# High and low half of the values side by side in attention's value product, on one Trainium2 core

## The reference, cut to what matters

```
q = rms_norm(x @ Wq + bq, gq).reshape(b, -1, n, d)        # b 8, 256 queries, n 16 heads, d 32
k_img = rms_norm(ctx_img @ Wk_img + bk_img, gk_img).reshape(b, -1, n, d)   # 256 keys
v_img = (ctx_img @ Wv_img + bv_img).reshape(b, -1, n, d)
probs = softmax(einsum('bqnd,bknd->bnqk', q, k_img) * scale)
img_x = einsum('bnqk,bknd->bqnd', probs, v_img)
out = img_x.reshape(b, -1, n * d) @ Wo + bo
```

## Time and profile before

| | |
|---|---|
| median of 3 executions | 1144.49 us (1142.92 to 1145.18) |
| profiled execution, its own time | 1142.49 us |
| its span, first to last instruction | 1140.7 us |
| mean granted TensorE clock | 0.942 |
| attention | about 490 to 712 us of the span |

### The profile page before, as it was taken

The page is one execution under the profiler, slowest core; times in us unless marked ns, Lnnn a source line. Parts: engine busy times, 40 slices in busy tenths (PEclk is TensorE's granted clock), DMA queues, the critical chain, the costliest instruction groups (busy, mean ns, idle before and its releaser), DMA issues. The chain is left out here.

```text
span 1140.7 us, 24592 instructions
## 1 busy us (share of the span) xinstructions
PE 1028.6 (90%) x9092; PEld 771.4 (68%) x9175; DVE 844.8 (74%) x1480; ACT 684.5 (60%) x1203; POOL 582.4 (51%) x635
## 2 busy tenths in 40 slices
PE   5899997789997998868999988789898899999997
PEld 5677775634443776457888766587675788888884
DVE  5589999779998788757888876598756555655548
ACT  4665773779986656567888864484444355545431
POOL 5444445424554445348888786303884355555520
PEclk9999999789999999969999999658999899999998
DMA  8584431869885223222222210564796477678879
GB/s 318 185 255 123 166 110 30 159 191 230 227 223 166 92 67 110 71 80 57 58 57 59 70 43 2 203 263 170 207 273 224 167 239 243 232 250 276 308 265 355
DMA packets 133705, 194.60 MB, mean 171 GB/s; under 512 B 67990, under 2 KB 70204, under 8 KB 132792
## 3 DMA queue, kind: packets, MB, share of 16 engines
q1 hardware_dynamic: 117256, 149.45, 42.5%
q0 software_dynamic: 8544, 24.68, 6.9%
q10 hardware_dynamic: 7792, 18.96, 5.1%
HBM read 127.47 MB, written 44.48 MB: 151 GB/s over the span
## 5 line engine op out<-in xcount | busy, mean ns | idle before, releaser
L470 PE MATMUL ps_y<-kv,toep 128*128 128x288 f32 x640 | 156.5, 407 | 3.2 <-DMA toep<-taps_padded 2.1
L470 PEld LDWEIGHTS ps_y<-kv,toep 128*128 128x128 f32 x640 | 121.2, 190 | 37.9 <-DMA toep<-taps_padded 3.5
L164 POOL TENSOR_TENSOR kv<-kx 128x1024 f32<-128x1024 f32 x32 | 60.6, 1895 | 83.7 <-DVE outT L524 37.6
L1798 DVE TENSOR_REDUCE at_negmax<-ps_s 128x4 f32<-128x1024 f32 x64 | 78.1, 1221 | 32.0 <-PE ps_s L1849 31.3
L2674 POOL DMA_INDIRECT expert_results<-e_yo,target x47 | 68.6, 1459 | 57.5 <-ACT e_yo L2725 57.5
L1141 PEld LDWEIGHTS ps_eg<-e_xT,e_w 128*128 128x128 bf16 x1128 | 69.0, 100 | 14.9 <-issue 2.4
L1141 PE MATMUL ps_eg<-e_xT,e_w 128*128 128x128 bf16 x1128 | 73.1, 223 | 3.8 <-DVE e_xT L2786 3.8
L1141 PE MATMUL ps_eu<-e_xT,e_w 128*128 128x128 bf16 x1128 | 71.5, 220 | 0.0
L2779 DVE COPY e_w<-expert_weights 128x4096 bf16 x47 | 57.7, 1227 | 17.9 <-issue 17.9
L2792 DVE SCALAR_TENSOR_TENSOR e_y<-ps_eu,e_bias,e_y 128x128 f32<-128x128 f32 x94 | 28.7, 347 | 55.5 <-PE ps_eu L1141 53.6
L2669 POOL DMA_INDIRECT e_rows<-token_rows,token x45 | 43.7, 971 | 50.4 <-PE ps_ex L2876 44.5
(11 more groups left out here) (450 smaller groups left out, 3089.0 us busy)
## 6 DMA issues: line engine op xcount, KB each, us to landing
e_parts<-down_parts SPq DMA_DIRECT2D x47, 512.0 KB
w_raw<-in_L_ffn_w ACTq DMA_DIRECT2D x32, 512.0 KB, 4.3
toep<-taps_padded SPq DMA_DIRECT2D x32, 256.0 KB, 3.6
f_draw<-in_L_ffn_rw SPq DMA_DIRECT2D x16, 512.0 KB, 4.3
down_parts<-f_dparts SPq DMA_DIRECT2D x16, 512.0 KB, 2.9
expert_weights<-expert_results SPq DMA_DIRECT2D x16, 512.0 KB, 11.1
x_res<-in_x SPq DMA_DIRECT2D x4, 1024.0 KB
c_in<-in_ctx SPq DMA_DIRECT2D x4, 1024.0 KB, 14.5
```

Source lines behind the costliest of these rows:

```text
L164: pool.tensor_tensor(pairs[:, :, :, 0:HD0], x[:, :, 0:HD0].unsqueeze(2).broadcast_to([P, ROWS_N, WIDE, HD0]), sliding_rows(x, 0, 1, WIDE), ...
L470: last = pe.matmul(y[:, l * B:(l + 1) * B, :, WIDE - 1:], toep[h % 2][:, (DC - 1 - l + m) * P:(DC - l + m) * P], kv[h % 2][:, m * B:(m + 1 ...
L1798: dve.tensor_reduce(negmax[u % 2][:, :].rearrange("p (j q) -> p j q", j=2), psS[:, :, :, :], AX.X, ALU.max, negate=True).then_inc(max_read, 1)
```

## The change

v_hi and v_lo become the two halves of one tile `v_parts` (per head 33 columns high, 33 columns low). The products ph by v_hi and ph by v_lo become one product of 66 columns into a wider ps_o (4 x 2 x 33); pl by v_hi goes into the high half alone. A unit has 8 products of 66 and 8 of 33 columns instead of 24 of 33. VectorE's scaling now covers both halves (4 x 2 x 32) and writes a float32 tile in SBUF, `o_halves`. A second tensor_tensor ("the add") waits for it and adds the two halves into o. TensorE waits for the scaling (`o_scaled`), and the turning of the output still waits for the last write into o (`o_read`).

```diff
-        psO = ctx.enter_context(nc.psum_tensor("ps_o", [P, 4, VC], F32))
+        psO = ctx.enter_context(nc.psum_tensor("ps_o", [P, 4, 2, VC], F32))
+        o_halves = sb("at_ohalves", [P, 4, 2, HD], F32)
...
-                    link(dve.reciprocal(rden[:, :], psO[:, :, HD]))
+                    link(dve.reciprocal(rden[:, :], psO[:, :, 0, HD]))
+                    dve.tensor_tensor(o_halves[:, :, :, :], psO[:, :, :, 0:HD],
+                                      rden[:, :].unsqueeze(2).unsqueeze(3).broadcast_to([P, 4, 2, HD]), ALU.mult).then_inc(o_scaled, 1)
+                    dve.wait_ge(o_scaled, g - 1)
                     out = o[ob % 2][:, :, uo * 2 * HD:(uo + 1) * 2 * HD].rearrange("p q (j d) -> p j q d", j=2)
-                    dve.tensor_tensor(out, psO[:, :, 0:HD].rearrange("p (j q) d -> p j q d", j=2),
-                                      rden[:, :].rearrange("p (j q) -> p j q", j=2).unsqueeze(3).broadcast_to([P, 2, 2, HD]),
-                                      ALU.mult).then_inc(o_read, 1)
+                    halves_of = lambda i: o_halves[:, :, i, :].rearrange("p (j q) d -> p j q d", j=2)
+                    dve.tensor_tensor(out, halves_of(0), halves_of(1), ALU.add).then_inc(o_read, 1)
...
                 if g:
-                    pe.wait_ge(o_read, g)
+                    pe.wait_ge(o_scaled, g)
                 for j in range(2):
                     for q in range(2):
                         cols = slice(q * P, (q + 1) * P)
-                        for n, (pr, vv) in enumerate(((ph, v_hi), (ph, v_lo), (pl, v_hi))):
-                            for kc in range(2):
-                                last = pe.matmul(psO[:, 2 * j + q, :], pr[u % 4][:, j, kc, cols], vv[:, b * 2 + kc, 2 * u + j, :],
-                                                 start=(n == 0 and kc == 0), stop=(n == 2 and kc == 1))
+                        for kc in range(2):
+                            pe.matmul(psO[:, 2 * j + q, :, :], ph[u % 4][:, j, kc, cols], v_parts[:, b * 2 + kc, 2 * u + j, :, :],
+                                      start=(kc == 0), stop=False)
+                        for kc in range(2):
+                            last = pe.matmul(psO[:, 2 * j + q, 0, :], pl[u % 4][:, j, kc, cols], v_parts[:, b * 2 + kc, 2 * u + j, 0, :],
+                                             start=False, stop=(kc == 1))
...
-                v_hi = left(attention, "v_hi", [P, NT, HEADS, VC], BF16)
-                v_lo = left(attention, "v_lo", [P, NT, HEADS, VC], BF16)
+                v_parts = left(attention, "v_parts", [P, NT, HEADS, 2, VC], BF16)
+                v_hi, v_lo = (v_parts[:, :, :, i, :] for i in range(2))
```

More of the change, by code:

```diff
@@ L1562, in normalise, with stage_attention @@
            .then_inc(self.xn_ready, 1)
-def stage_attention(k, ks, last_keys, v_hi, v_lo, qw, ow, vectors, x_mean, x_rstd, stats, qs, kb, ahead, front):
+def stage_attention(k, ks, last_keys, v_parts, qw, ow, vectors, x_mean, x_rstd, stats, qs, kb, ahead, front):
     nc = k.nc
@@ L1608, in stage_attention @@
         maxes_high, ones_copied, bias_zeroed, bias_high, bias_low, shift_ready = (sem(n) for n in ("mxh", "oc", "bz", "bh", "bw", "xs"))
-        stacked, k_loaded = sem("st"), sem("kl")
+        stacked, k_loaded, o_scaled = (sem(n) for n in ("st", "kl", "os"))
         block = ctx.enter_context(nc.Block())
@@ L3007, in build @@
                                  lambda name: ctx.enter_context(nc.semaphore(name)))
-            stage_attention(k, ks, (k_hi[(len(ITEMS) - 1) % 2], k_lo[(len(ITEMS) - 1) % 2]), v_hi, v_lo, qw, ow, k.vectors, x_mean, x_rstd, stats, qs, kb, ahead, front)
+            stage_attention(k, ks, (k_hi[(len(ITEMS) - 1) % 2], k_lo[(len(ITEMS) - 1) % 2]), v_parts, qw, ow, k.vectors, x_mean, x_rstd, stats, qs, kb, ahead, front)
             k.retired_stack.close()
```

## The result

| | median | executions |
|---|---|---|
| before | 1144.84 us | 4 (1142.92 to 1145.56) |
| changed | 1201.14 us | 4 (1199.15 to 1203.31) |

By medians the change costs 56.3 us, where the prediction had 60.5.

The account below looks back on a forecast made before the run. Attention, bound by TensorE, becomes bound by VectorE with GpSimd: 142.3 + 101.5 + 3.0 + 5.4 us plus some 3 of waits, 255 for 195. With 0.5 at the end, 1142.5 + 60.5 = 1203 profiled, median 1205; range 1172 to 1226 us.

Parts of the forecast that it names:

- The add is held by the subtraction in nearly all steps: In attention, VectorE's add waits for GpSimd's subtraction in all steps but two per batch, VectorE held 2.16 us longer.
- It starts 0.06 us ahead: GpSimd's subtraction starts at 611.36, 0.06 us before VectorE's add at 611.42, so the add loses.
- The add ends 0.15 us after the subtraction: In a locked step the add's visible rest after the subtraction's end is about 0.15 us, ending at 613.41.
- The two other steps per batch: Where queries are prepared, six batches: add free at u = 7, 0.5 us more; next step 0.9 us more.
- The sum: VectorE's time over 59 attention steps, with the add's holds and some waits: 255 us in place of 195, +60 us.
- VectorE becomes the bound, with TensorE near 73%: VectorE with GpSimd bounds attention; a batch takes about 34.7 us with TensorE busy near 73%.
- The rival of the clock: TensorE's clock falls too, at 1.2 GHz binding for ten units: +20 us, 1225 us; chance 7%.
- That is the whole possible gain here, and it is one only while TensorE is the bound: TensorE's value products in attention take 0.18 us less per unit, 11.5 us over 64 units.
- The first step of the prediction: Busy time per attention batch: TensorE busy 26.57 of 27.10 us, so attention is bound by TensorE.
- 0.66 us per unit: VectorE's free time in attention, from 5.3 us per batch of eight units; VectorE work is free up to it.
- The rival of the add that slips in: The add gets in between L1674 and the subtraction in every step: about 1137 us, faster; chance 8%.
- the 0.028 I took: TensorE's time in us for a 66-column value product, from 256 columns taking 0.11 us.

Follow-up runs that it names:

- the cure by a PSUM input: Changed kernel with the high half scaled in place in ps_o, so one input of the add is in PSUM: 1144.8 us, 1.0048 to the kernel before.
- order: Changed kernel with GpSimd starting a step's subtraction only after that step's add: 1148.0 us, 1.0080 to the kernel before.
- 0.2 us of earliness: Changed kernel with the reciprocal left out, VectorE scaling by ones: 1143.9 us, 1.0036 to the kernel before.
- the cut: Changed kernel with GpSimd's subtraction cut into two instructions of 512 elements: 1158.6 us, 1.0172 to the kernel before.
- the part alone: Kernel before with 66-column products, VectorE scaling only the high half, low half's sums left out: 1136.2 against 1139.0 us, 0.9980.
- the sums without folds: Kernel before without the three folds of squares per batch, TensorE summing the four chunks itself: 1.0152.

## Why the prediction was right, and where it was not

- **The add is held by the subtraction in nearly all steps: shown.** It follows from the trace, from the cure by a PSUM input (1.0048), by order (1.0080) and by 0.2 us of earliness (1.0036), and from the cut (1.0172). With one input in PSUM the add is free even where it starts 0.12 us behind the subtraction. "It starts 0.06 us ahead": 0.051 to 0.059 us in the ordinary locked steps. "The add ends 0.15 us after the subtraction": 0.145 to 0.148 us. Of the 59 adds in the stretch, 45 are locked, where 47 were counted: in two more the subtraction came 0.08 us after the add, and the add won (0.29 us).
- **The two other steps per batch: right.** At u = 7 the add takes 0.29 us. At u = 0 it takes 0.70 us in five of the six batches (1.05 in the first), is through 0.87 us later than the scaling before (0.9 forecast), and gets in between two GpSimd instructions.
- **The sum.** From 502.88 to 698.13, 255 us were forecast for the new stretch; it is 249.1, so +53.9 in place of +60. Scaling, gap and add together take 106.3 us more than the scaling did (96.3 + 25.1 - 17.2, and 59 gaps of 0.036), against 109.9 forecast: that is the two locked steps fewer. Another 3.5 us are overlap that was not counted: by the groups, VectorE's instructions sum to 13.8 us more than its busy time, 10.3 before, as more of them follow each other without a gap. The other way, VectorE's idle time outside the gaps before the adds was put at 3 us and is 5.2 (7.3 less 2.1). The profiled span grew by 60.9 us all the same, since 3.5 us more passed before the stretch and 3.6 behind it. All fourteen profiled kernels, which compute the same ahead of it, reach this point between 502.9 and 507.0 us, so this is spread from execution to execution, and the close hit of the total owes some us to it.
- **VectorE becomes the bound, with TensorE near 73%.** VectorE yes; TensorE shows 80% over the stretch of 34.5 us. The clock explains only 2 points of that: the granted clock is 0.95 there, and in the batch at 1.00 TensorE is busy for 26.81 of 34.45 us, 78%. The other 5 points are a wrong sum: 0.18 us per unit were taken off the busy time of 26.57 us, and it rose instead. TensorE's instructions overlap in the records (177 ns long, 25.5 ns apart), so where they stand in shorter runs with waits between them the same work shows more busy time; that is my reading of it, and no run tests it. The rival of the clock had the fall right (0.91 over the 59 steps, 0.98 before) and its price wrong: the batch at 1.00 takes 34.45 us and the one before it, at 0.95, 34.49. The middle batches take 34.45 to 35.20 us against 34.7 forecast.
- **"That is the whole possible gain here, and it is one only while TensorE is the bound": the size was wrong by five.** The unit's products save 0.165 us (0.18 forecast), but the part alone gains 0.2%, some 2 us and not clear of nothing, in place of 11.5. The first step of the prediction failed here: "Attention is bound by TensorE", read from a busy share of 98% over a batch. The table of steps shows that u = 6, 7, 2 and 3 are as long with less TensorE work. VectorE has 0.45 us free at u = 6, 0.03 at u = 7 and 0.33 at u = 0, so the "0.66 us per unit" of free time, a mean over the batch, doesn't exist there. At u = 0, 0.29 of the 0.33 us is a wait for TensorE, and this step did get shorter. In the other full steps a third engine is close: from 602.1 to 617.7 us of the kernel before (u = 7 to u = 3) GpSimd never idles for more than 0.17 us at a time. Whether it holds u = 2 and u = 3 was not tested.
- **The rival of the add that slips in had the wrong sign.** It was priced at 1137 us, faster. Made to happen, it is 1.0036 to 1.0080, slower. It was worked out from batch averages (25.5 against 27.1 us). By steps, of the 0.46 us of new VectorE work 0.30 show at u = 6 and 0.47 at u = 7: with the subtraction after the add they take 4.91 and 3.28 us, in place of 4.61 and 2.81. In both of these runs some adds are still held (at u = 0 and 3), but in the run with an input in PSUM none is, and it is 1.0048. So no form of this change that ran is a gain, even with the lock gone. The chance given for faster, 0.06, rested on that error.

The pace of the wide product, on the timeline of TensorE (pairs of products, starts):

```profile
619.12 0.22 PE L1876 MATMUL ps_o<-v_parts,kw 128*128 128x66 bf16 x2
619.18 0.21 PE L1879 MATMUL ps_o<-v_parts,vw 128*128 128x33 bf16 x2
619.23 0.22 PE L1876 MATMUL ps_o<-v_parts,kw 128*128 128x66 bf16 x2
```

Two wide and two narrow ones take 0.11 us, so with 0.0255 for a narrow one a wide one takes 0.030 us, not the 0.028 I took. For 66 columns the rule of the Trainium skill (TensorE: Matmul & The Clock Gate, Back-to-back issue gap) gives 30 ns, and the trace sides with it.

What stays open: why every second batch waits at u = 5 for the queries' transfer once TensorE is faster, and which engine holds u = 2 and u = 3. Neither was tried.

## What to carry to other kernels

Before an instruction is added to VectorE, look at where its inputs lie and at what GpSimd does at that moment: two SBUF inputs beside a long GpSimd instruction cost nearly its whole rest here (1.99 against 0.29 us), and with one input in PSUM that wait was gone. A busy share of 98% over several steps doesn't name the bound of each: list the steps by their length and see which engine has no gap in each. When an experiment moves work off an engine to free it, look up in its trace what the work costs where it went: the sums without folds cost TensorE 1.34 us, and hid the answer. When a race of 0.05 us decides over 5%, force the order rather than hope for it.

## What the runs showed of the hardware

- An add of 128 elements per partition from SBUF and SBUF takes 0.291 us, or 1.99 us when a GpSimd tensor_tensor of 1.90 us started 0.055 us before it. With one input in PSUM its longest of 64 is 0.293 us. In the last steps one lost by 0.017 us (2.02 us long). Near a tie the recorded start does not decide: without the reciprocal one add starts 0.002 us before a subtraction by the trace (525.49 us) and is held all the same, 2.04 us long.
- It works the other way too: where VectorE was 0.08 us ahead, GpSimd's subtraction took 1.97 us in place of 1.90, and its L1675 0.36 in place of 0.22 us where both started together.

```profile
544.51 0.29 DVE L1810 TENSOR_TENSOR at_o<-at_ohalves 128x128 f32<-128x128 f32 x1
544.58 1.97 POOL L1688 TENSOR_TENSOR vw<-kw 128x1024 bf16<-128x1024 f32 x1
```

- A waiting VectorE instruction gets in between two GpSimd instructions issued back to back (1.13 us with the subtraction in two halves).
- TensorE's product of one f32 column shows as two records 0.112 us apart (sums of the squares: 16 records in 1.92 us, 4 in 0.58), where one of 33 bf16 columns takes 0.0255 us.
